# Alternating two score passes of an attention stage pass by pass, and drawing its first projections into the stage before

## Chip, cores, metric

One NeuronCore of a Trainium2 chip runs the whole program. The metric is the device time of one execution in microseconds (us); where a number below is a time on the trace, it counts from the start of the span.

## What is computed

`x` is 32 sequences of 64 tokens of width 128, `ctx_1024` has the same shape. Two decoder layers, each an attention block, a cross attention block and a feed-forward block, each with a residual and a layer norm:

```python
x = _layernorm(x + _L0_attn_ref(x, ...))        # stage 0, a state-space mixer
x = _layernorm(x + _L0_xattn_ref(ctx_1024, ctx_1024, x, ...))   # stage 1
x = _layernorm(x + _L0_ffn_ref(x, ...))         # stage 2, routed experts
x = _layernorm(x + _L1_attn_ref(x, ...))        # stage 3, window attention
x = _layernorm(x + _L1_xattn_ref(x, ctx_1024, ...))   # stage 4
x = _layernorm(x + _L1_ffn_ref(x, ...))         # stage 5, routed experts
```

Stage 4, which the change is about:

```python
def _L1_xattn_ref(x, mem, Wq, Wkv, Wout, bout):     # 16 heads of depth 8, mem = ctx_1024
    q = x @ Wq
    xc = jnp.concatenate((mem, x), axis=1)          # 64 + 64 keys
    k, v = jnp.split(xc @ Wkv, 2, axis=-1)
    dots = jnp.einsum('bhid,bhjd->bhij', q, k) * scale      # per head
    dots = jnp.where(j_idx > i_idx + mem_len, -jnp.inf, dots)
    out = jnp.einsum('bhij,bhjd->bhid', softmax(dots), v)
    return out @ Wout + bout
```

## The kernel before

Activations lie transposed in SBUF (128 features on the partitions, 2048 tokens along them). Each engine has its own hand-written instruction order, and semaphores tie the engines together. Stages 0 to 3 go over four chunks of 512 tokens: `run` calls a `front` for a chunk, which is handed the norm pieces of the chunk before (`hook`) and early pieces of the chunk after (`nxt`). Stage 4 goes over 16 pairs of sequences (`PAIRS`) and 8 halves of a chunk (`HALVES`, four sequences each), one pair per iteration `i` of the loops `stage4` that PE, ACT and DVE each have.

What PE does for a pair `k` in stage 4, with its lines:

- `scores4(k, half)`: queries on the output partitions. Depth is 8, so four heads share a group `g` of 32 partitions; a matmul has 32 rows (group `g`) and 64 output columns (L2097, float32, 256 elements moved). Half 0 takes groups 0 and 1, half 1 groups 2 and 3; both write banks 0 and 1. Eight matmuls of 32 x 32 in bf16 then add the mask (L2104). DVE takes the row maxima (`maxima4`, L1418), splits them in two bf16 parts (`split4`), PE turns them (`turn4`, L2148), ACT copies them.
- `scores_by_key4(k)`: the same scores once more, keys on the output partitions, 32 rows and 128 columns each (L2116, float32, 256 elements moved), groups 0 to 3, banks 2, 3, 5, 6; eight masks of 32 x 32 (L2122, bf16, 512 elements).
- `less_max4(k)` (L2130) takes the maxima off, ACT's `exps4` (L852) makes the exponentials, `pv4(k)` (L2158, L2162) multiplies with the values and sums.
- Once in two iterations each: `k_project4` (L2070) and `q_project4` (L2074), or `v_project4` (L2080). ACT copies the keys (`k_copy4`, L831) and spreads them by head (`k_by_head4`, L837, four activations).

Each float32 matmul stands in the trace as two passes, so a count x16 is eight matmuls. An iteration of PE before:

```python
for i in range(PAIRS + 2):
    scores4(i, 0); scores_by_key4(i - 1)
    k_project4(i // 2 + 1) or v_project4(i // 2)
    q_project4(i // 2 + 1)          # even i
    scores4(i, 1); less_max4(i - 1); pv4(i - 2); turn4(i)
```

`k_project4` and `pv4` share bank 4, so `pv4` waits in an even iteration until ACT has copied the keys; and `k_copy4(h)` itself waits for `s_t4` of `4 * (2 * h - 2)`, that is until `less_max4(i - 1)` of the same iteration, since the two halves in `k4` are by then still being read. `s_t4` counts the last `less_max4` matmul of each group.

Stage 4 opens on PE with the last norm pieces of stage 3 (`tail3`: L2054, L2057), then `k_project4(0)`, `q_project4(0)`; ACT then copies and spreads the keys, and DVE fills `xcat` (`inputs4`) and copies the queries (`q_copy4`). `keep_warm` is six plain bf16 matmuls without use (L2169). POOL sets the value and maxima buffers to zero (L567, L568) and spreads the queries by head (L576).

Of the kernel before, what the change touches and what calls it, by code (L numbers as in the profile page):

```python
# [24 lines left out]
P = 128  # L25
# [17 lines left out]
def _program(nc, ctx, dram, out, where_c, where_w):  # L43
# [115 lines left out]
    def run(eng, fronts, pres, tails):  # L159
# [3 lines left out]
        for front, pre, tail in zip(fronts, pres, tails):  # L163
# [3 lines left out]
            front(NCH - 1, lambda part: tail(NCH - 2, part), nothing)  # L167
# [187 lines left out]
    xcat = take(2 * CHUNK).rearrange("p (b i t) -> p b i t", b=SEQS, i=2)  # L355
# [5 lines left out]
    vx4 = vx4_all.rearrange("p (b j g r) -> p b j g r", b=SEQS, j=4, g=4)  # L361
    max4_all = take(2 * SEQ)
    max4 = max4_all.bitcast(BF16).rearrange("p (i g r) -> p i g r", i=2, g=4)
    maxT4 = [take(SEQ).bitcast(BF16) for _ in range(2)]
# [14 lines left out]
    by_key = [bank[n] for n in (2, 3, 5, 6)]  # L379

# [110 lines left out]
    def _(pool):  # L491
# [73 lines left out]
        def stage4():  # L565
            pool.wait_ge(s_w2, 9 * NCH)
            pool.memset(vx4_all, 0.0).then_inc(s_z4, 1)  # L567
            pool.memset(max4_all, 0.0).then_inc(s_z4, 1)  # L568
            pool.wait_ge(s_wvs, 3 * NCH)
# [10 lines left out]
        run(pool, [front0, front1, front2, front3], [no_pre, no_pre, no_pre, pre3], [tail0, tail1, tail2, tail3])  # L580
# [3 lines left out]
    def _(act):  # L584
# [243 lines left out]
        def k_copy4(h):  # L828
            wait(act, s_k4, h + 1)
            wait(act, s_t4, 4 * (2 * h - 2))  # L830
            act.activation(k4[:, half_rows(h), :], bank[4][:].rearrange("p (b t) -> p b t", b=4), ACT.Copy).then_inc(s_kx4, 1)  # L831

        def k_by_head4(h):
            wait(act, s_kx4, 5 * h + 1)
            wait(act, s_s4, 2 * (2 * h - 2))
            for j in range(4):
                act.activation(kx4[:, half_rows(h), j, :], k4[:, half_rows(h), :], ACT.Copy, scale=const("inner")[:, j:j + 1])\  # L837
# [10 lines left out]
        def exps4(k):  # L848
            wait(act, s_pv4, k - 1)
            for g in range(4):  # L850
                wait(act, s_t4, 4 * k + g + 1)
# [6 lines left out]

        def stage4(hook):
            act.wait_ge(s_z4, 2)  # L860
            k_copy4(0)
            k_by_head4(0)
            hook(1)
            for i in range(PAIRS + 2):
# [7 lines left out]
                if i in VAR_AT4:  # L872
                    tail4(VAR_AT4[i], 2)
                if 1 <= i <= PAIRS:
# [3 lines left out]
                if i in OUT_AT:  # L878
                    tail4(OUT_AT[i], 1)
# [79 lines left out]
        stage5(stage4(run(act, [front0, front1, front2, front3], [no_pre, pre1, pre2, pre3], [tail0, tail1, tail2, tail3])))  # L959
# [1590 lines left out]
```

## Time and profile before

| what | value |
|---|---|
| time of three runs, median (lowest to highest) | 873.44 us (872.77 to 874.19) |
| time of the profiled execution | 873.73 us |
| its span, first to last instruction | 871.9 us |
| granted TensorE clock, mean over the span | 0.968 |
| PE busy | 785.4 us, 90% of the span |
| DVE busy | 492.0 us, 56% |
| ACT busy | 404.9 us, 46% |
| POOL busy | 110.6 us, 13% |
| share of PE in the chain that ended last | 70% |
| stage 3 / stage 4 / stage 5 begin near | 447 / 538 / 693 us |

The profiled execution is 1.8 us longer than its span and 0.3 us above the median. Busy time of PE adds overlapping passes once only; matmuls on different tiles of the array run beside each other, so the mean time of one pass times their number is more than the busy time.

### The profile page before, as it was taken

What the parts mean: (1) busy time and instruction counts of PE and PEld (TensorE: products, weight loads), DVE (VectorE), ACT (ScalarE), POOL (GpSimd) and SP (SyncE); (2) the same over time, 40 slices, a digit from 0 to 9 for tenths busy, and PEclk for the clock granted to TensorE, in tenths of its full rate; (3) what the DMA queues carried; (4) which work ended last, traced back from release to release, by engine and by line L of the source; (5) the groups of instructions that cost most, each with busy time, mean ns of one, the idle gap of its engine ahead of it and who ended that gap; (6) DMA issues with size and microseconds to landing.
All of it is one profiled execution on the core that took longest, in us unless ns stands there. A gap on an engine that the chain in (4) does not pass through costs nothing.

```text
span 871.9 us, 17126 instructions
## 1 busy us (share of the span) xinstructions
PE 785.4 (90%) x6680; PEld 396.7 (45%) x6681; DVE 492.0 (56%) x1166; ACT 404.9 (46%) x735; POOL 110.6 (13%) x107
## 2 busy tenths in 40 slices
PE   6999999997988869999986867899999899999996
PEld 4445354444555533433324444455656544443332
DVE  1543323324888876566448773365666466646662
ACT  3737354554566652333431332355545344554454
POOL 1270221211000000000003445121110000000000
PEclk9999999999899998999997998899999899999998
DMA  9400000000000000000000000000000000000000
GB/s 359 170 2 1 1 0 0 1 2 1 2 2 1 1 2 0 0 1 0 0 1 1 1 0 0 2 3 3 3 3 3 2 0 1 1 1 0 13 12 24
DMA packets 2372, 13.51 MB, mean 15 GB/s; under 512 B 256, under 2 KB 256, under 8 KB 1664
## 3 DMA queue, kind: packets, MB, share of 16 engines
q1 hardware_dynamic: 2304, 12.56, 3.6%
q8 instruction: 47, 0.77, 0.3%
q14 instruction: 21, 0.17, 0.1%
HBM read 11.51 MB, written 1.05 MB: 14 GB/s over the span
## 4 chain that ended last, share of the span: by engine, by line
PE 70%; DVE 13%; ACT 8%; issue 7%; DMA 1%; DVEq 0%; POOL 0%; ACTq 0%; SPq 0%
PE bank L1726 6%; PE bank L2097 4%; PE bank L2338 4%; PE bank L1952 3%; PE bank L2264 3%; PE bank L1764 3%; PE bank L2317 3%; PE bank L2274 3%; PE bank L1777 3%; PE bank L1968 3%; PE bank L1957 3%; PE bank L2116 2%; PE bank L2158 2%; PE bank L121 2%; DVE sb_rowmax L1099 2%
## 5 line engine op out<-in xcount | busy, mean ns | idle before, releaser
L1726 PE MATMUL bank<-sb_xT,sb_arena 128*128 128x512 f32 (+1 forms) x128 | 63.1, 626 | 3.5 <-ACT sb_arena L605 2.5
L1418 DVE TENSOR_REDUCE sb_rowmax<-bank 128x4 f32<-128x512 f32 x64 | 41.1, 684 | 33.8 <-PE bank L2104 33.1
L605 ACT ACTIVATE sb_arena<-bank 128x512 f32<-128x512 f32 x64 | 37.4, 597 | 37.6 <-PE bank L1726 37.5
L1030 DVE TENSOR_TENSOR sb_arena<-bank,sb_arena 128x512 f32<-128x512 f32 x32 | 22.1, 690 | 50.2 <-PE bank L1777 49.9
L757 ACT ACTIVATE sb_arena<-bank 128x512 f32<-128x512 f32 x36 | 21.4, 596 | 55.6 <-PE bank L1952 54.1
L513 POOL TENSOR_TENSOR sb_arena<-sb_la,sb_consts 128x1024 f32<-128x1024 f32 x16 | 30.6, 1920 | 112.2 <-PE bank L1764 88.8
L1952 PE MATMUL bank<-sb_xT,sb_w 128*128 128x512 f32 (+1 forms) x72 | 40.7, 648 | 0.0
L1726 PEld LDWEIGHTS bank<-sb_xT,sb_arena 128*128 128x128 f32 x128 | 22.4, 194 | 37.3 <-ACT sb_arena L605 21.9
L852 ACT ACTIVATE sb_arena<-bank 128x512 f32<-128x512 f32 x64 | 33.0, 605 | 13.3 <-PE bank L2130 13.3
L2097 PE MATMUL bank<-sb_arena 32*64 32x256 f32 x512 | 35.8, 395 | 3.0 <-ACT sb_arena L837 2.9
L1646 DVE TENSOR_TENSOR sb_arena<-sb_arena,bank 128x512 f32<-128x512 f32 x32 | 21.0, 683 | 29.7 <-PE bank L2321 22.0
L1957 PE MATMUL bank<-sb_xT,sb_w 128*128 128x512 f32 (+1 forms) x72 | 37.7, 605 | 0.0
L1968 PE MATMUL bank<-sb_arena,sb_w 128*128 128x512 f32 x72 | 37.6, 614 | 0.0
L648 ACT ACTIVATE sb_arena<-bank 128x512 f32<-128x512 f32 x32 | 18.7, 597 | 39.1 <-PE bank L1764 39.0
L1311 DVE TENSOR_TENSOR sb_arena<-sb_arena,bank 128x512 f32<-128x512 f32 x32 | 21.9, 686 | 25.0 <-PE bank L1957 16.3
L714 ACT ACTIVATE sb_arena<-sb_arena 128x512 f32<-128x512 f32 x32 | 20.1, 630 | 33.0 <-DVE sb_arena L1104 33.0
L1863 PE MATMUL bank<-sb_arena 128*64 128x256 f32 x256 | 34.5, 398 | 0.7 <-ACT sb_arena L672 0.5
L2338 PE MATMUL bank<-sb_arena,sb_w 128*128 128x512 f32 x64 | 34.9, 635 | 0.0
L918 ACT ACTIVATE sb_arena<-bank,sb_w 128x512 f32<-128x512 f32 x32 | 21.3, 687 | 27.4 <-PE bank L2317 27.4
L2041 PE MATMUL bank<-sb_arena,sb_consts 128*128 128x128 f32 x192 | 25.3, 294 | 8.3 <-POOL sb_arena L546 6.6
L1764 PE MATMUL bank<-sb_arena,sb_consts 128*128 128x512 f32 x64 | 32.7, 592 | 0.0
L2317 PE MATMUL bank<-sb_xT,sb_w 128*128 128x512 f32 x64 | 32.3, 597 | 0.0
(344 smaller groups left out, 1640.3 us busy)
## 6 DMA issues: line engine op xcount, KB each, us to landing
sb_w<-w SPq DMA_DIRECT2D x1, 2646.5 KB, 25.6
sb_consts<-consts SPq DMA_DIRECT2D x1, 1812.0 KB, 14.4
sb_w<-w SPq DMA_DIRECT2D x1, 1736.0 KB, 19.4
sb_w<-w SPq DMA_DIRECT2D x1, 1175.0 KB, 9.2
sb_arena<-w SPq DMA_DIRECT2D x2, 512.0 KB, 4.1
sb_ctxT<-ctx SPq DMA_DIRECT2D x1, 1024.0 KB, 16.4
out<-sb_xT SPq DMA_DIRECT2D x4, 256.0 KB, 2.5
sb_xT<-x SPq DMA_DIRECT2D x1, 768.0 KB, 10.6
```

Of the source, the lines that this page charges most:

```text
L605: act.activation(V[:, h, :], bank[h % 2][:], ACT.Copy).then_inc(s_vev, 1)
L852: act.activation(probT4[k % 2][:, g].rearrange("p b j q -> p (b j q)"), by_key[g][:], ACT.Exp).then_inc(s_e4, 1)
L1418: dve.tensor_reduce(rowmax4[k % 2][:, 4 * g:4 * g + 4], bank[n][:].rearrange("p (j t) -> p j t", j=4), AX, ALU.max).then_inc(s_mx4, 1)
L1726: pe.matmul(bank[h % 2][:], KT[:, h, :], cols(c), start=True, stop=True).then_inc(s_v, 1)
L1764: pe.matmul(bank[2 + half][:], const("later"), decay[k % 2][:, 8 * half:8 * half + 8, :].rearrange("p h t -> p (h t)"), start=False, stop= ...
L1863: mm = pe.matmul(bank[2 + u % 3][64 * b:64 * b + 64, 256 * gg:256 * gg + 256], qg[:, 2 * (u % 2) + gg, q:q + SEQ], kx[:, 2 * k + b].rearra ...
L1952: pe.matmul(bank[n % 2][:], w1v[:, i, :], cols(c), start=True, stop=True).then_inc(s_g2, 1)
L1957: pe.matmul(bank[2 + n % 2][:], w3v[:, i, :], cols(c), start=True, stop=True).then_inc(s_u2, 1)
L1968: pe.matmul(bank[5][:], w2v[:, (n - 3) % 9, :], hid[(n - 2) % 3], start=(n == 2), stop=(n == 10))\
L2097: mm = pe.matmul(scored[64 * b:64 * b + 64, :, at], q4[rows(g), q:q + SEQ], kx4[rows(g), b0 + b, :, at], start=(part == 0), stop=True, ski ...
L2317: pe.matmul(up_bank(c, i)[:], f1v[:, i, :], cols(c), start=True, stop=True).then_inc(s_f1, 1)
L2338: pe.matmul(bank[3][:], f2v[:, i, :], hid5[i % 4], start=(i == 0), stop=False).then_inc(s_f2, 1)
```

## The change

Four things. (1) `scores_by_key4(k)` is gone; `scores4(i, half)` now issues the pair `i` in the one form and the pair `i - 1` in the other, in turn: for each of two parts, four matmuls of 32 x 64 on two row groups, then two of 32 x 128 on the other two row groups. The masks of both follow. (2) The keys have three buffers instead of two halves of one, and `k_copy4` waits for an older `less_max4`. (3) `k_project4(0)`, `q_project4(0)`, their copies and both `inputs4` stand in the last chunk of stage 3, and `scores4(0, 0)` ahead of `tail3`; POOL's zeroing stands in the first chunk of stage 3. (4) Buffers move so that this is free of overlaps; the orders of groups for masks, `less_max4` and `exps4` become 2, 3, 0, 1; `tail4(.., 1)` on ACT stands ahead of `exps4`.

```diff
-            front(NCH - 1, lambda part: tail(NCH - 2, part), nothing)
+            front(NCH - 1, lambda part: tail(NCH - 2, part), opening if front is fronts[-1] else nothing)
...
-    k4 = take(SEQS * P).rearrange("p (b t) -> p b t", b=SEQS)
+    k4 = [ap.rearrange("p (b t) -> p b t", b=4) for ap in (take(4 * P), sb("k4_second", [P, 4 * P])[:], sb("k4_third", [P, 4 * P])[:])]
...
+    KEY_GROUPS = (2, 3, 0, 1)
+    projected_q4 = [bank[6], bank[5]] + [bank[7]] * (2 * NCH - 2)
...
@@ POOL, front3, first chunk @@
+                pool.wait_ge(s_w2, 9 * NCH)
+                pool.memset(vx4_all, 0.0).then_inc(s_z4, 1)
+                pool.memset(max4_all, 0.0).then_inc(s_z4, 1)
                 pre3(0, 4)
@@ ACT @@
         def k_copy4(h):
             wait(act, s_k4, h + 1)
-            wait(act, s_t4, 4 * (2 * h - 2))
-            act.activation(k4[:, half_rows(h), :], bank[4][:].rearrange("p (b t) -> p b t", b=4), ACT.Copy).then_inc(s_kx4, 1)
+            wait(act, s_t4, 4 * (2 * h - 4))
+            act.activation(k4[h % 3], bank[4][:].rearrange("p (b t) -> p b t", b=4), ACT.Copy).then_inc(s_kx4, 1)
...
+        def opening4(piece):
+            if piece == 3:
+                k_copy4(0)
+                k_by_head4(0)
@@ DVE @@
+        def opening4(piece):
+            if piece == 0:
+                inputs4(0)
+            if piece == 2:
+                q_copy4(0)
+            if piece == 3:
+                inputs4(1)
@@ PE @@
         def scores4(k, half):
-            groups = (2 * half, 2 * half + 1)
-            b0 = 2 * (k % 4)
-            wait(pe, s_kx4, 5 * (k // 2) + 5)
-            wait(pe, s_qc4, k // 2 + 1)
-            wait(pe, s_mx4, 4 * k + 2 * half)
+            groups, key_groups = (2 * half, 2 * half + 1), KEY_GROUPS[2 * half:2 * half + 2]
+            b0, e0 = 2 * (k % 4), 2 * ((k - 1) % 2)
+            if k < PAIRS:
+                wait(pe, s_kx4, 5 * (k // 2) + 5)
+                wait(pe, s_qc4, k // 2 + 1)
+                wait(pe, s_mx4, 4 * k + 2 * half)
+            if k > 0:
+                wait(pe, s_kx4, 5 * ((k - 1) // 2) + 1)
+                wait(pe, s_qx4, 4 * ((k - 1) // 2) + 4)
+                wait(pe, s_e4, 4 * (k - 1) - 2 + 2 * half)
             for part in range(2):
                 at = slice(SEQ * part, SEQ * part + SEQ)
+                if k < PAIRS:
+                    for g in groups:
...
+                            pe.matmul(scored[64 * b:64 * b + 64, :, at], q4[rows(g), q:q + SEQ], kx4[rows(g), b0 + b, :, at],
+                                      start=(part == 0), stop=True, skip_group_check=(part == 1))
+                if k > 0:
+                    for g in key_groups:
+                        pe.matmul(by_key[g][:, 256 * part:256 * part + 256], k4[(k - 1) // 2 % 3][rows(g), e0 + part, :],
+                                  qx4[rows(g), 2 * ((k - 1) % 4) + part].rearrange("p j q -> p (j q)"), start=(part == 0),
+                                  stop=True, skip_group_check=(part == 1))
...
         def turn4(k):
             wait(pe, s_mb4, 2 * k + 2)
+            if k == 0:
+                wait(pe, s_resid, 4 * NCH)
...
+        def opening4(piece):
+            if piece == 1:
+                pe.wait_ge(s_w[4], 16)
+                pe.wait_ge(s_c3, 3 * NCH)
+                k_project4(0)
+                q_project4(0)
...
         def stage4(hook):
-            hook(0)
...
             for i in range(PAIRS + 2):
-                if i < PAIRS:
+                if i <= PAIRS:
                     scores4(i, 0)
-                if 1 <= i <= PAIRS:
-                    scores_by_key4(i - 1)
+                if i == 0:
+                    hook(0)
```

**The order on PE, iteration 3 of stage 4.** The names in it: L2097 is a score matmul of 32 x 64, L2104 its mask, L2116 a by-key matmul of 32 x 128, L2122 its mask, L2080 the value projection, L2130 `less_max4`. Before:

```order
L2097 MATMUL bank<-sb_arena 64x4x64 x8
L2104 MATMUL bank<-sb_consts 32x4x64 x8
L2116 MATMUL bank<-sb_arena 128x256 x8
L2122 MATMUL bank<-sb_consts 32x512 x8
L2080 MATMUL bank<-sb_w,sb_arena 128x128 x4
L2097 MATMUL bank<-sb_arena 64x4x64 x8
L2104 MATMUL bank<-sb_consts 32x4x64 x8
L2130 MATMUL bank<-sb_arena,sb_consts 128x2x64 x16
L2158 MATMUL bank<-sb_arena 32x64 x32
L2162 MATMUL bank<-sb_arena,sb_consts 32x128 x16
```

In the changed kernel the same stretch reads as follows (L2115 is the score matmul, L2119 the by-key one, L2126 and L2135 their masks, L2091 the value projection):

```order
L2115 MATMUL bank<-sb_arena 64x4x64 x4
L2119 MATMUL bank<-sb_arena,sb_k_second 128x256 x2
L2115 MATMUL bank<-sb_arena 64x4x64 x4
L2119 MATMUL bank<-sb_arena,sb_k_second 128x256 x2
L2126 MATMUL bank<-sb_consts 32x512 x4
L2135 MATMUL bank<-sb_consts 32x4x64 x8
L2091 MATMUL bank<-sb_w,sb_arena 128x128 x4
L2115 MATMUL bank<-sb_arena 64x4x64 x4
L2119 MATMUL bank<-sb_arena,sb_k_second 128x256 x2
L2115 MATMUL bank<-sb_arena 64x4x64 x4
L2119 MATMUL bank<-sb_arena,sb_k_second 128x256 x2
L2126 MATMUL bank<-sb_consts 32x512 x4
```

The matmuls are the same in number. The eight by-key matmuls that stood in one run behind the first half now stand in four runs of two, each between runs of four score matmuls, and the shape changes with each run.

**The order on PE where stage 3 ends.** Before, from the last chunk's norm pieces on (L2041 spreads window weights, L121 is the variance, L2054 and L2057 are `tail3`, L2070 and L2074 the first projections):

```order
L2054 MATMUL bank<-sb_xT,sb_consts 128x512
L2057 MATMUL bank<-sb_arena,sb_w 128x512 x3
L2041 MATMUL bank<-sb_arena,sb_consts 128x128 x24
L121 MATMUL bank<-sb_sq,sb_consts 128x512
L2054 MATMUL bank<-sb_xT,sb_consts 128x512
L2057 MATMUL bank<-sb_arena,sb_w 128x512 x3
L2070 MATMUL bank<-sb_arena,sb_w 128x512
L2074 MATMUL bank<-sb_xT,sb_w 128x256
L2097 MATMUL bank<-sb_arena 64x4x64 x8
L2104 MATMUL bank<-sb_consts 32x4x64 x8
```

And in the change (L2052 spreads the window weights, L2065 and L2068 are `tail3`, L2081 and L2085 the projections):

```order
L2068 MATMUL bank<-sb_arena,sb_w 128x512 x3
L2052 MATMUL bank<-sb_arena,sb_consts 128x128 x12
L2081 MATMUL bank<-sb_arena,sb_w 128x512
L2085 MATMUL bank<-sb_xT,sb_w 128x256
L2052 MATMUL bank<-sb_arena,sb_consts 128x128 x12
L121 MATMUL bank<-sb_sq,sb_consts 128x512
L2115 MATMUL bank<-sb_arena 64x4x64 x8
L2135 MATMUL bank<-sb_consts 32x4x64 x8
L2065 MATMUL bank<-sb_xT,sb_consts 128x512
L2068 MATMUL bank<-sb_arena,sb_w 128x512 x3
L2081 MATMUL bank<-sb_arena,sb_w 128x512
L2085 MATMUL bank<-sb_xT,sb_w 128x256
```

The two projections moved to the middle of the window weights of the last chunk, and the first scores ahead of `tail3`.

**The order on ACT there.** Before (L126, L135, L138 are norm pieces, L831 copies the keys, L837 spreads them):

```order
L126 ACTIVATE sb_sq<-sb_resid 128x512
L135 ACTIVATE sb_lnv<-bank,sb_eps_ln 128x512
L138 ACTIVATE sb_rstd<-sb_lnv 128x512
L831 ACTIVATE sb_arena<-bank 128x512
L837 ACTIVATE sb_arena<-sb_arena,sb_consts 128x4x128 x4
L126 ACTIVATE sb_sq<-sb_resid 128x512
L831 ACTIVATE sb_arena<-bank 128x512
```

In the change (L834 copies the keys, L840 spreads them):

```order
L126 ACTIVATE sb_sq<-sb_resid 128x512
L834 ACTIVATE sb_arena<-bank 128x512
L840 ACTIVATE sb_arena<-sb_arena,sb_consts 128x4x128 x4
L135 ACTIVATE sb_lnv<-bank,sb_eps_ln 128x512
L138 ACTIVATE sb_rstd<-sb_lnv 128x512
L126 ACTIVATE sb_sq<-sb_resid 128x512
L834 ACTIVATE sb_k_second<-bank 128x512
```

Copy and spreading of the first keys moved ahead of the norm of the last chunk but one.

## Rows read from the trace of the kernel before

**Rows 1.** The page: busy time by engine, share of the span, instructions
```profile
PE 785.4 (90%) x6680; PEld 396.7 (45%) x6681; DVE 492.0 (56%) x1166; ACT 404.9 (46%) x735; POOL 110.6 (13%) x107
```

**Rows 2.** Busy time of the engines 588 to 680 us, PE PEld DVE ACT POOL, clock, DMA
```profile
588.00:680.00 92.00, 88.11 (x2124) 56.46 (x2119) 55.72 (x109) 47.49 (x109) 9.31 (x16) 1.00 0.01 3
```

**Rows 3.** The chain over two iterations of stage 4: start us, us, what
```profile
585.10 0.61 ACT sb_arena L831
...
585.75 1.10 PE bank L2158 x64
...
587.88 1.02 PE bank L2097 x16
588.90 0.23 PE bank L2104 x8
589.13 1.07 PE bank L2116 x16
590.21 0.34 PE bank L2122 x8
590.55 1.09 PE bank L2080 x8
591.64 1.02 PE bank L2097 x16
...
597.96 1.06 PE bank L2070 x2
599.02 0.43 PE bank L2074 x2
```

**Rows 4.** Timeline of PE, where shapes change: start us, us, engine, line, output and inputs
```profile
588.29 0.61 PE L2097 MATMUL bank<-sb_arena 32*64 32x256 f32 x8
588.83 0.30 PE L2104 MATMUL bank<-sb_consts 32*32 32x256 bf16 x8
...
592.59 0.30 PE L2104 MATMUL bank<-sb_consts 32*32 32x256 bf16 x8
592.82 0.40 PE L2130 MATMUL bank<-sb_arena,sb_consts 32*128 32x128 bf16 x16
```

**Rows 5.** Timeline of PE, 548 to 600 us, six useless bf16 matmuls
```profile
551.30 1.47 PE L2169 MATMUL bank<-sb_consts 128*128 128x512 bf16 x6
```

**Rows 6.** Waits from 553 to 680 us: who waited for whom, total us, times, longest
```profile
PE bank L2158 <- ACT sb_arena L831: 5.0, 6, 0.8
```

**Rows 7.** Timeline of DVE, the maxima of one half
```profile
589.21 1.29 DVE L1418 TENSOR_REDUCE sb_rowmax<-bank 128x4 f32<-128x512 f32 x2
```

**Rows 8.** Timeline of all engines, 515 to 548 us, end of stage 3, start of stage 4
```profile
526.15 5.52 PE L2041 MATMUL bank<-sb_arena,sb_consts 128*128 128x128 f32 x48
...
533.31 1.13 PE L2054 MATMUL bank<-sb_xT,sb_consts 128*128 128x512 f32 x2 [0.78 <-ACT sb_lnv L135]
...
534.27 2.74 PE L2057 MATMUL bank<-sb_arena,sb_w 128*128 128x512 f32 x6
...
538.35 1.10 PE L2070 MATMUL bank<-sb_arena,sb_w 128*128 128x512 f32 x2 [1.34 <-DVE sb_arena L1404]
...
539.54 0.60 ACT L831 ACTIVATE sb_arena<-bank 128x512 f32<-128x512 f32 x1 [5.62 <-PE bank L2070]
...
540.17 2.56 ACT L837 ACTIVATE sb_arena<-sb_arena,sb_consts 128x512 f32<-128x512 f32 x4
...
542.78 1.98 PE L2097 MATMUL bank<-sb_arena 32*64 32x256 f32 x16 [2.91 <-ACT sb_arena L837]
```

**Rows 9.** Timeline of PE, 548 to 600 us, second run of scores
```profile
550.04 1.09 PE L2097 MATMUL bank<-sb_arena 32*64 32x256 f32 x16
```

**Rows 10.** Timeline, POOL's zeroing, and DVE's products without and with POOL busy
```profile
533.68 3.52 POOL L567 MEMSET sb_arena<- 128x4096 f32 x1
...
449.23 3.70 DVE L1343 TENSOR_TENSOR sb_arena<-sb_arena 128x512 f32<-128x512 f32 x6 [1.66 <-ACT sb_arena L779]
...
464.26 6.30 DVE L1343 TENSOR_TENSOR sb_arena<-sb_arena 128x512 f32<-128x512 f32 x6 [1.91 <-ACT sb_arena L779]
```

More of the change, by code:

```diff
@@ L157, in is_last, with run @@
         return isinstance(c, int) and c == NCH - 1
-    def run(eng, fronts, pres, tails):
+    def run(eng, fronts, pres, tails, opening):
         hook = nothing
@@ L354, in _program @@
     attn4 = [take(CHUNK), sb("attn4_odd", [P, CHUNK])[:]]
-    xcat = take(2 * CHUNK).rearrange("p (b i t) -> p b i t", b=SEQS, i=2)
+    maxT4 = [take(SEQ).bitcast(BF16) for _ in range(2)]
+    take = carve(11840)
     q4 = take(CHUNK)
     qx4 = take(4 * CHUNK).rearrange("p (b j q) -> p b j q", b=SEQS, j=4)
-    k4 = take(SEQS * P).rearrange("p (b t) -> p b t", b=SEQS)
+    k4 = [ap.rearrange("p (b t) -> p b t", b=4) for ap in (take(4 * P), sb("k4_second", [P, 4 * P])[:], sb("k4_third", [P, 4 * P])[:])]
     kx4 = take(SEQS * 4 * P).rearrange("p (b j t) -> p b j t", b=SEQS, j=4)
@@ L361, in _program @@
     vx4 = vx4_all.rearrange("p (b j g r) -> p b j g r", b=SEQS, j=4, g=4)
+    xcat = take(2 * CHUNK).rearrange("p (b i t) -> p b i t", b=SEQS, i=2)
     max4_all = take(2 * SEQ)
     max4 = max4_all.bitcast(BF16).rearrange("p (i g r) -> p i g r", i=2, g=4)
-    maxT4 = [take(SEQ).bitcast(BF16) for _ in range(2)]
     rden4 = rms_l[:, 0:P]
@@ L579, in _ @@
         setup_pool()
-        run(pool, [front0, front1, front2, front3], [no_pre, no_pre, no_pre, pre3], [tail0, tail1, tail2, tail3])
+        run(pool, [front0, front1, front2, front3], [no_pre, no_pre, no_pre, pre3], [tail0, tail1, tail2, tail3], nothing)
         stage4()
@@ L849, in exps4 @@
             wait(act, s_pv4, k - 1)
-            for g in range(4):
-                wait(act, s_t4, 4 * k + g + 1)
+            for n, g in enumerate(KEY_GROUPS):
+                wait(act, s_t4, 4 * k + n + 1)
                 act.activation(probT4[k % 2][:, g].rearrange("p b j q -> p (b j q)"), by_key[g][:], ACT.Exp).then_inc(s_e4, 1)
@@ L873, in stage4 @@
                     tail4(VAR_AT4[i], 2)
+                if i in OUT_AT:
+                    tail4(OUT_AT[i], 1)
                 if 1 <= i <= PAIRS:
@@ L958, in _ @@
         setup_act()
-        stage5(stage4(run(act, [front0, front1, front2, front3], [no_pre, pre1, pre2, pre3], [tail0, tail1, tail2, tail3])))
+        stage5(stage4(run(act, [front0, front1, front2, front3], [no_pre, pre1, pre2, pre3], [tail0, tail1, tail2, tail3], opening4)))
     @block.vector
@@ L1693, in _ @@
         setup_dve()
-        stage5(stage4(run(dve, [front0, front1, front2, front3], [no_pre, pre1, pre2, pre3], [tail0, tail1, tail2, tail3])))
+        stage5(stage4(run(dve, [front0, front1, front2, front3], [no_pre, pre1, pre2, pre3], [tail0, tail1, tail2, tail3], opening4)))
     @block.tensor
@@ L2095, in scores4 @@
                     for b in range(2):
[L2096 to L2124 removed]
+                        for h in range(2):
+                            o = 64 * b + 32 * h
+                            mm = pe.matmul(scored[o:o + 32, :, SEQ:], eye32[rows(g)],
+                                           late_key[rows(g), h].unsqueeze(1).to_broadcast([32, 4, SEQ]), start=False, stop=True,
+                                           skip_group_check=True)
+                mm.then_inc(s_s4, 1)
         def less_max4(k):
@@ L2128, in less_max4 @@
             for j in range(4):
-                for g in range(4):
+                for g in KEY_GROUPS:
                     mm = pe.matmul(by_key[g][:].rearrange("p (b j q) -> p b j q", b=2, j=4)[:, :, j, :],
@@ L2386, in _ @@
         setup_pe()
-        stage5(stage4(run(pe, [front0, front1, front2, front3], [no_pre, pre1, pre2, pre3], [tail0, tail1, tail2, tail3])))
+        stage5(stage4(run(pe, [front0, front1, front2, front3], [no_pre, pre1, pre2, pre3], [tail0, tail1, tail2, tail3], opening4)))
 def _layouts(np, a):
```

69 lines of the change are left out of this document (18 added, 51 removed).

## Prediction

> **What bounds the kernel now.** I read the page first: PE is busy for 90% of the span, DVE for 56% [rows 1], and the page's chain that ended last lies on PE for most of its length. Then the steady part of stage 4 alone, 588 to 680 us: PE busy 88.1 of 92 us at the full granted clock, DVE 55.7, ACT 47.5 [rows 2]. So what the change does to PE's own time there counts in full. The chain over two iterations [rows 3] shows the pieces end to end: score run 1.02, its masks 0.23, by-key run 1.07, its masks 0.34, a projection, the second score run 1.02. The one wait of any size is ACT's copy of the keys, 0.61.
>
> **What a run of small matmuls is made of.** Two passes of 256 elements in float32 that follow without a change of shape take 0.43, the last row of [rows 3], so a pass streams in 0.215. The 16 passes of the score run are four rounds on four tiles (two row groups, two column halves): 0.86, and 0.16 over. The by-key run is four rounds on four row groups: 0.86, and 0.21 over [rows 3]. Six plain bf16 passes of 512 elements take 1.47 including the tail of the last [rows 5], about 0.22 each; so the eight masks of 256 elements (0.11) and of 512 (0.22) all run beside each other and leave 0.12 over in 0.23 and 0.34 [rows 3]. Every run pays 0.12 to 0.21 for being a new shape.
>
> **Does a change of shape wait for tiles that it doesn't use?** This decides the case. At 592.59 the masks are on row groups 2 and 3. The next shape, 32 x 128, begins with group 0, which nothing had used since before the run at 591.64, yet it starts 0.23 after the masks, just as late as the by-key run behind the masks of half 0 (588.83 to 589.07), which needs the tiles that they hold [rows 4]. The eight take 0.30 together, most of it the way through the array; the last starts 0.02 after the first and streams for 0.11, so the new shape starts 0.10 after the whole array is through. I looked at every change of shape in the trace, several hundred: none starts earlier than about 0.09 after the stream before it ends. The Trainium skill, page TensorEngine Tiling (Array Packing), section Key Properties, has the same: changing the tiling mode, not merely the tile, drains TensorE. By that rule the trace agrees, and it speaks against this change.
>
> **Term 1, the alternated passes.** A half of `scores4` in iterations 1 to 15 is now two parts of: eight score passes, two rounds on four tiles, 0.43 + 0.16 = 0.59; then four by-key passes, two rounds on two tiles, 0.43 + 0.21 = 0.64. Half of the four row groups stand idle in each run. Both sets of masks are 32 x 32 and go together: 0.34. A half is 2 x (0.59 + 0.64) + 0.34 = 2.80, a pair 5.60. Before, a pair was 1.02 + 0.23 + 1.07 + 0.34 + 1.02 + 0.23 = 3.91 [rows 3], 62.6 for 16 pairs. Now: the first iteration has scores alone, 2 x 1.25 = 2.5; fifteen mixed ones, 84.0; iteration 16 has by-key alone but in two runs, 2 x (0.86 + 0.21 + 0.34) = 2.8. Sum 89.3, **+26.7**. Nothing hides it, since PE is the bound.
>
> **Term 2, the third key buffer.** The copy of the keys waited for `less_max4` and `pv4` for the copy, six times, 5.0 us idle [rows 6]. Now the copy only needs the projection, 2 us or more ahead, and ACT is free then. **-5.0.** The wait that could come in its place is the exponentials of the pair before; they follow `less_max4` at 0.6 each (the copy of that shape takes 0.60 [rows 8]), and the first two are asked for only after both runs of `pv4`, the first of which alone takes 1.10 [rows 3], and `turn4`: no wait.
>
> **Term 3, less cover for the maxima.** The second half of a pair writes the banks that DVE reads for the first. The maxima end 1.67 after the first mask starts (588.83 to 590.50) [rows 4, 7]; with twelve masks and the semaphore I take 1.85. By-key matmuls used to lie between the halves; now there is 0.34 for the masks and a projection: 1.09 in odd iterations, 1.06 + 0.43 in even ones [rows 3]. So odd iterations wait 0.4, even ones not. Most odd ones have a norm piece there; iterations 3 and 5 have none. **+0.9.** Behind that wait on PE stand the second half, `less_max4` and `turn4`, so it counts in full.
>
> **Term 4, the opening.** Before, the first scores start at 542.78, behind `tail3`, the projections, the copy (0.60) and four spreading activations (2.56) [rows 8]. Now the projections stand in the middle of L2041, whose 48 passes take 5.52 from 526.15: after 24 of them, 528.9. They delay the second 24 by 1.06 + 0.43 = 1.5; L121 then ends near 533.9. ACT starts the copy near 529.9 and is done near 533.1, ahead of that. So the first scores start near 534.0 at the full clock: 8.8 earlier. From there to the second run of scores PE had 7.3 (542.78 to 550.04 [rows 8, 9]), part of it at the lower clock (the first run took 1.98 for the usual 1.02). Now: scores and masks 1.25, `tail3` 1.0 + 2.6, without the last pass's tail [rows 8], projections 1.5, `keep_warm` 1.4 [rows 5] and some 0.15 of waits: 7.9. Net **-8.1**. Bounds: -9 (no stretch at the lower clock and no waits) and -3 (DVE's value products, the copy of the queries and two `inputs4` pile up in the last chunk, or the new order brings a lower clock itself). I take the value from the added rows; it is nearest to them.
>
> **Term 5, POOL's zeroing** (3.52) moves to 446 us, beside the first products of stage 3. Six of those took DVE 3.70 alone and 6.30 with POOL busy [rows 10]; some 1.5 us of overlap at that rate would cost 0.6; a memset reads nothing, so it may cost 0: **+0.5**, bounds 0 and 1.5. The old place of the zeroing was beside PE's work: no gain. The extra buffers, the order of groups and the place of `tail4(.., 1)` cost nothing: same instructions, and ACT has half its time free.
>
> **Sum.** The profiled execution took 873.7 (span 871.9 and 1.8 around it), 0.3 above the median. 26.7 - 5.0 + 0.9 - 8.1 + 0.5 = +15.0, so 888.7 against the execution, **888.4** against the median.
>
> **Rivals.** (a) *Tiles of different shape do overlap when their row groups are disjoint.* The group orders 2, 3, 0, 1 are laid out for it. A half would be four rounds with one change, 0.86 + 0.21, and 0.34: 1.41. A pair 2.82; stage 4's runs 2.5 + 15 x 2.82 + 2.8 = 47.6, -15.0, and with the other terms -26.7: **846.7**. It decides if a by-key pass starts within some 0.03 of the score pass issued ahead of it. The same page and section of the Trainium skill says that different tiles can load and multiply in parallel; both rules are stated and the trace shows each, the second only within one shape. For it: nothing but that no float32 pair of shapes on disjoint groups is in the trace. Against: rows 5. Chance 0.15. (b) *A change between 32 x 64 and 32 x 128 is cheap*, since both have 32 rows: it waits for the stream but the 0.16 and 0.21 shrink to the 0.10 that follows every stream. 120 runs, some 0.08 less each: -9, **879**. Chance 0.08. (c) *The opening pays little, or the emptier array brings the lower clock back.* At the lower clock a stretch costs as much again as it takes (the run of scores 1.98 for 1.02 [rows 8, 3]); a stretch of some 7 us more at that clock costs 3.5, the opening at its bound another 5: **893 to 897**. Chance 0.15. (d) Gains and losses cancel: 0.02.
>
> **How the numbers follow.** Forecast 0.60, its own span 883 to 893. A measurement of this kernel can tell 0.2% (1.7 us) from no change. Faster is (a) and a little of (d), 0.16; within 0.2% 0.02; slower all else, 0.82. The range 875 to 899 holds the forecast, (b), (c); outside lie (a), (d) and 0.03 of tails.
>
> **What would show it.** The score passes in fours and the by-key passes in twos, each run starting only when the one before is through: a by-key run 0.59 after the score run, the next score run 0.64 later, a half 2.8 long. An even and an odd iteration together some 2.6 longer than before (3.4 more for two pairs, 0.8 less for one copy). ACT's copy of the keys gone from the chain. First scores near 534, the second run near 542. It is wrong if by-key passes start inside the score run's rounds, or if other stages move by over 1 us.

## The result, and the profile after

| | before | after |
|---|---|---|
| device time, median (lowest to highest) | 873.82 us (872.77 to 877.2), 4 runs | 897.89 us (895.27 to 901.77), 4 runs |
| profiled execution / its span | 873.73 / 871.9 us | 895.27 / 893.5 us |
| granted TensorE clock, mean over the span | 0.968 | 0.968 |
| PE busy | 785.4 us, 90% | 811.1 us, 91% |

The ratio is 1.0272, with a 95% interval of 1.0224 to 1.0321: slower by 2.7%. The forecast was 888.4 with a range to 899; the median lies inside it, 9.5 above the forecast. It lies outside the forecast's own span of 883 to 893, and also above the 893 to 897 of rival (c). The profiled execution is the fastest of the four; the other three took 896.71, 899.08 and 901.77 us with clocks of 0.963, 0.963 and 0.960.

The page of the changed kernel, busy time by engine (to be read beside [rows 1]):

```profile
PE 811.1 (91%) x6680; PEld 402.2 (45%) x6681; DVE 493.5 (55%) x1166; ACT 405.8 (45%) x735; POOL 111.0 (12%) x107
```

PE gained 25.7 us of busy time with the same instructions; DVE, ACT and POOL did not move. So most of the added time is not PE waiting for another engine: the same passes of PE lie less beside each other.

The chain of waits of the changed kernel over an odd and the following even iteration (start us, us, what), beside [rows 3]:

```profile
569.90 0.64 issue
570.53 0.66 PE bank L2115 x8
...
575.77 0.59 PE bank L2115 x8
576.37 0.63 PE bank L2119 x4
577.00 0.59 PE bank L2115 x8
577.59 0.63 PE bank L2119 x4
578.22 0.22 PE bank L2126
578.44 0.02 PE bank L2135 x7
...
578.47 1.13 PE bank L2081 x2
...
580.03 0.13 issue
```

The same half by the starts of its matmuls, from the timeline of PE:

```profile
575.70 0.66 PE L2115 MATMUL bank<-sb_arena 32*64 32x256 f32 x8
576.29 0.70 PE L2119 MATMUL bank<-sb_arena,sb_k_second 32*128 32x256 f32 x4
```

The next two runs start at 576.93 and 577.52, the masks at 578.15 and the projection at 578.47. A half is 0.59, 0.63, 0.59, 0.63 and 0.32 for the masks, 2.77 in all against a forecast of 2.80, and so, within 0.01, is every other half between 565 and 675 us. (The chain starts a piece where the one before ends, at 575.77, so it shows 2.70 and 0.25 for the masks, and 0.66 for the first run of a half that follows a wait.) Where [rows 3] had one score run of 1.02 and one by-key run of 1.07, there are now four runs, each of which begins when the one before is through. The `issue` piece of 0.64 at 569.90 is new: the second half of the pair waits there until DVE has read the banks that it will write (DVE's side is in the rows below).

Timeline of the changed kernel, DVE and PE around that wait (start us, us, engine, line, output and inputs, idle time before and its releaser):

```profile
568.93 1.29 DVE L1424 TENSOR_REDUCE sb_rowmax<-bank 128x4 f32<-128x512 f32 x2 [1.55 <-PE bank L2135]
...
570.53 0.66 PE L2115 MATMUL bank<-sb_arena 32*64 32x256 f32 x8 [0.64 <-issue]
```

DVE reads the first half's scores from 568.93 to 570.22. The value projection (568.74 to 569.90) covers the first 0.97 of that, and the second half starts 0.3 after DVE's end. Here the first half is followed by nothing but the projection; before, the by-key run stood there too.

Timeline of the changed kernel at the end of stage 3 and the opening of stage 4, beside [rows 8, 9]:

```profile
527.40 1.02 PE L2081 MATMUL bank<-sb_arena,sb_w 128*128 128x512 f32 x2
...
529.09 2.56 ACT L840 ACTIVATE sb_arena<-sb_arena,sb_consts 128x512 f32<-128x512 f32 x4
...
532.32 1.09 PE L2115 MATMUL bank<-sb_arena 32*64 32x256 f32 x16
...
539.79 1.09 PE L2115 MATMUL bank<-sb_arena 32*64 32x256 f32 x16
```

The projections stand in the middle of the window weights, and ACT has copied and spread the keys by 531.65, before PE asks for them. The first scores start at 532.32 for 542.78 before, the second run at 539.79 for 550.04. That is 10.25 earlier, of which 1.81 is older: stage 3 itself began at 444.87 instead of 446.68. The opening paid 8.4, of which 3.4 is the stretch at the lower clock that it had before.

The granted clock of stretches of the changed kernel (window, its length, busy time of PE, PEld, DVE, ACT and POOL, clock, DMA):

```profile
543.00:553.00 10.00, 8.34 (x103) 3.96 (x103) 3.32 (x8) 6.67 (x15) 0.00 (x0) 1.00 0.00 1
553.60:560.40 6.80, 6.80 (x39) 2.65 (x37) 1.29 (x2) 0.60 (x1) 0.00 (x0) 0.50 0.01 2
588.00:680.00 92.00, 89.91 (x1753) 49.41 (x1749) 45.61 (x89) 41.20 (x92) 9.31 (x16) 0.98 0.01 3
683.30:690.10 6.80, 6.80 (x137) 4.31 (x137) 1.64 (x4) 2.06 (x4) 0.00 (x0) 0.50 0.01 2
```

Two stretches of 6.8 us ran at 0.50, that is at 1.2 GHz, and one of 3.4 us more lies inside 588 to 680. Both long ones follow idle time of PE: 1.7 of the 10 us before 553, and a wait of 1.73 at 680.2. The short one, at 608.2, does not: PE was busy for 4.73 of the 5 us ahead of it. Before, the stretch from 588 to 680 ran at 1.00 throughout [rows 2]; a stretch like the long ones lay in the opening, where the run of scores took 1.98 [rows 8], and a short one in iteration 2:

```profile
563.20:566.60 3.40, 3.40 (x23) 1.28 (x16) 0.85 (x2) 0.00 (x0) 0.00 (x0) 0.50 0.00 0
```

### The profile page after: what moved, and what is told of

Its sections match the earlier page's. It is cut to its first block, busy times and chain, and to the rows that moved or that the text cites. A ratio compares the mean times of both kernels' runs of the same rounds, so it can differ in the third digit from the quotient of the medians.

```text
span 893.5 us, 17165 instructions
## 1 busy us (share of the span) xinstructions
PE 811.1 (91%) x6680; PEld 402.2 (45%) x6681; DVE 493.5 (55%) x1166; ACT 405.8 (45%) x735; POOL 111.0 (12%) x107
## 4 chain that ended last, share of the span: by engine, by line
PE 69%; DVE 15%; issue 8%; ACT 7%; DMA 1%; DVEq 0%; POOL 0%; ACTq 0%; SPq 0%
PE bank L1737 6%; PE bank L2119 5%; PE bank L2115 4%; PE bank L2354 4%; PE bank L1963 3%; PE bank L2280 3%; PE bank L1775 3%; PE bank L2333 3%; PE bank L2290 3%; PE bank L1788 3%; PE bank L1979 3%; PE bank L1968 3%; DVE sb_rowmax L1105 2%; PE bank L121 2%; PE bank L2269 2%
## 5 line engine op out<-in xcount | busy, mean ns | idle before, releaser
L760 ACT ACTIVATE sb_arena<-bank 128x512 f32<-128x512 f32 x36 | 21.4, 596 | 55.7 <-PE bank L1963 54.1
L2115 PE MATMUL bank<-sb_arena 32*64 32x256 f32 x512 | 42.7, 406 | 4.2 <-issue 3.0
L2052 PE MATMUL bank<-sb_arena,sb_consts 128*128 128x128 f32 x192 | 25.9, 297 | 9.3 <-POOL sb_arena L550 7.6
L579 POOL TENSOR_TENSOR sb_arena<-sb_arena,sb_consts 128x256 f32<-128x256 f32 x32 | 19.1, 628 | 115.0 <-PE bank L2144 112.3
```

The costliest lines, as they stand in the source:

```text
L2115: pe.matmul(scored[64 * b:64 * b + 64, :, at], q4[rows(g), q:q + SEQ], kx4[rows(g), b0 + b, :, at], start=(part == 0), stop=True, skip_gro ...
```

## The experiments

All times are compared with runs of the kernel before on the same chip: 873.03 us (13 runs, 868.45 to 876.57) for the first four, 873.92 us (11 runs, 868.36 to 877.13) for the others. Diffs are against the changed kernel.

**1. The same passes in one shape.** Does the change of shape cost the time, or the alternation? The by-key matmul of 128 columns is cut into two of 64, so that it has the shape of the score matmul. There are 256 passes more, and no change of shape before the masks of a half.

```diff
                     for g in key_groups:
-                        pe.matmul(by_key[g][:, 256 * part:256 * part + 256], k4[...][rows(g), e0 + part, :], ...)
+                        for u in range(2):
+                            pe.matmul(by_key[g][64 * u:64 * u + 64, 256 * part:256 * part + 256],
+                                      k4[...][rows(g), e0 + part, 64 * u:64 * u + 64], ...)
```

> The changed kernel, but each by-key matmul of 32 x 128 is cut into two of 32 x 64, so scores and by-key passes have one shape and still lie on disjoint row groups; twice as many by-key passes. Theory (the price is the change of shape, and tiles of one shape overlap across all row groups): a mixed half is four rounds on eight tiles and one mask run, 0.86 + 0.16 + 0.05 + 0.34 = 1.4 us instead of the 2.77 of the changed kernel, 30 halves: 41 us less than the changed kernel's 898, about 857 us, ratio to before 0.98. Rival (no more than four passes stream at a time whatever their tiles): 32 passes in eight rounds, 2.2 us a half, about 881 us. Rival (disjoint row groups don't overlap at all): 3 us a half and over, 905 us or more.

Measured: 855.86 us (854.14 to 859.63), ratio 0.9818 (0.9764 to 0.9872): 42 us faster than the changed kernel and 17 faster than the one before, as the theory had it. Both rivals are out. Timeline of PE in this kernel, one half (L2115 is a score pass, L2120 a by-key pass):

```profile
576.27 0.45 PE L2115 MATMUL bank<-sb_arena 32*64 32x256 f32 x4
576.30 0.45 PE L2120 MATMUL bank<-sb_arena,sb_k_third 32*64 32x256 f32 x4
576.54 0.40 PE L2115 MATMUL bank<-sb_arena 32*64 32x256 f32 x4
576.57 0.39 PE L2120 MATMUL bank<-sb_arena,sb_k_third 32*64 32x256 f32 x4
...
577.32 0.39 PE L2128 MATMUL bank<-sb_consts 32*32 32x512 bf16 x4
...
577.65 1.16 PE L2091 MATMUL bank<-sb_w,sb_arena 128*128 128x128 f32 x8
```

The by-key passes start 0.03 after the score passes, inside their round, and the next round of four and four comes 0.27 later. All eight tiles stream together. A half takes 1.38, from 576.27 to 577.65, against 2.77 with two shapes. Of the 20 halves between 568 and 645 us 14 take 1.38; the other six hold pauses of PE and take 1.69 to 2.37. The data, the row groups, the banks and the order are the same; the only thing changed is that a tile has 64 columns and not 128 (and that there are two passes for one). This is the rival (a) of the prediction in all but its premise: the row groups do overlap, but only in one shape. In the words of the Trainium skill, page TensorEngine Tiling (Array Packing), section Key Properties, different tiles can run in parallel, and changing the tiling mode drains TensorE; the runs agree with both, and show that the second comes first.

**2. Fewer changes of shape.** Per half all score passes, then all by-key passes: one change inside a half where there were three.

```diff
-                if k > 0:
+            if k > 0:
+                for part in range(2):
                     for g in key_groups:
                         pe.matmul(by_key[g][:, 256 * part:256 * part + 256], ...
```

> The changed kernel, but inside a half all score passes go first and then all by-key passes: two runs of small matmuls instead of four, still on half of the row groups each. Theory: 1.02 + 1.07 + 0.34 = 2.43 us a half instead of 2.77, 30 halves, 10 us less than the changed kernel: about 888 us, ratio 1.016. Rival (the changes of shape themselves are cheap and the idle row groups are the whole price): 897 us, no difference from the changed kernel.

Measured: 892.65 us (892.04 to 893.41), ratio 1.0239 (1.0192 to 1.0285). The chain of this kernel shows the two runs of a half in place of four:

```profile
590.66 1.09 PE bank L2115 x16
591.75 1.06 PE bank L2120 x8
592.82 0.22 PE bank L2127
```

1.09 and 1.06, that is 2.15 for the 2.44 of the four runs (0.59, 0.63, 0.59, 0.63). An even iteration takes 9.15 (from one `turn4` to the next) against 9.87, which is 0.36 less per half. Over 30 halves that is 10.8 us, but the median fell by 5.2 only. The rest is in the clock:

```profile
553.80:570.90 17.10, 16.62 (x194) 9.34 (x198) 5.14 (x12) 3.94 (x10) 2.33 (x4) 0.50 0.01 2
```

17.1 us at 1.2 GHz in one stretch, where the changed kernel had 6.8 in that place. That costs (17.1 - 6.8) / 2, some 5 us more. So the price of a change of shape is confirmed as such (the rival expected no difference), and half of what two fewer of them gave was taken back by the clock. Why this order has more of the lower clock stays open.

**3. The by-key run whole again.** The alternation alone is undone: eight by-key matmuls in one run behind half 0, with their masks and waits, as before. The opening and the third key buffer stay.

```diff
+            if k > 0 and half == 0:
+                for part in range(2):
+                    for g in key_groups:
+                        pe.matmul(by_key[g][:, 256 * part:256 * part + 256], ...
...
-                if i <= PAIRS:
+                if i < PAIRS:
                     scores4(i, 1)
```

> The changed kernel, but the by-key pass is one run over all four row groups behind the first half's scores and masks again, as before the change; the opening, the third key buffer and everything else of the change stay. Theory: the alternation costs all of the loss, so this is faster than before by the opening (8 to 10 us) and the key copy (some 4 of its 5 us, the rest goes to the wait for the maxima ahead of the turn in even iterations): 859 to 862 us, ratio 0.985. Rival (the opening or the new key buffers are part of the loss): 870 us or more.

**4. The same, and the old wait of the copy.** On top of run 3 the copy of the keys waits again for the `less_max4` of the same iteration.

```diff
-            wait(act, s_t4, 4 * (2 * h - 4))
+            wait(act, s_t4, 4 * (2 * h - 2))
```

> As whole_key_run, with the copy of the keys waiting for the same less_max4 as before the change. Theory: the six waits of 0.9 us for ACT's copy come back, less the 0.2 each that the maxima would have cost: 4 us more than whole_key_run, 864 to 866 us, ratio 0.990. Rival (the third buffer saves nothing, as another wait is as late): the same time as whole_key_run within 1 us.

Measured: run 3 took 860.78 us (858.89 to 863.22), ratio 0.9863 (0.9816 to 0.991), and run 4 took 867.5 us (859.37 to 869.8), ratio 0.9926 (0.9891 to 0.996). Run 3 is as expected; run 4 lies 1.5 above its 864 to 866, and its intervals with run 3 overlap a little, so their difference is read from the profiled executions below (867.1 and 863.22). Both are faster than before, so the alternation alone is what made the change slower: it accounts for 37 us between run 3 and the changed kernel, more than the whole loss. (It brings with it the shorter cover for the maxima of term 3.) Some 30 of them are the passes and the waits for the maxima (steps 1 and 3 below), and 8 the clock: run 3's spans at 0.971 miss 24.9 us of it, the changed kernel's at 0.963 miss 33.

The difference of 3 and 4 is the third key buffer. The chain of run 4 in an even iteration:

```profile
595.43 0.61 ACT sb_k_second L834
...
596.08 1.10 PE bank L2175 x64
```

and that of run 3 in the same place:

```profile
596.77 0.40 DVE sb_arena L1435
...
597.20 0.55 DVE sb_arena L1437
...
597.79 0.23 PE bank L2165
```

In run 4 ACT's copy of 0.61 stands on the chain, as in [rows 3]. In run 3 it is gone, and DVE's split of the maxima stands there (L1435, L1437), for which `turn4` waits. An even iteration takes 8.72 in run 4, as before, and 8.06 in run 3: 0.66 gained of the 0.83 that the copy cost (5.0 over six [rows 6]). The split is slow just there. Timeline of run 3, DVE and POOL:

```profile
595.95 2.33 POOL L579 TENSOR_TENSOR sb_arena<-sb_arena,sb_consts 128x256 f32<-128x256 f32 x4 [13.14 <-PE bank L2145]
...
596.77 0.39 DVE L1435 CAST sb_arena<-sb_rowmax 128x16 bf16<-128x16 f32 x1
597.20 0.54 DVE L1437 TENSOR_TENSOR sb_arena<-sb_rowmax,sb_arena 128x16 bf16<-128x16 f32 x1
```

The two small instructions take 0.39 and 0.54 while POOL spreads the queries (L579); in odd iterations, without POOL, they take 0.17 each. The kernel before had the same slow pair in its even iterations (0.39 and 0.54), hidden behind the wait for the copy. The Trainium skill, page GPSIMD Engine Reference, section Specifications, says that POOL and DVE share their access to SBUF, and contend where a DVE instruction has two SBUF inputs or runs in a 2-port mode; L1437 has two inputs and grew most. L1435 has one and more than doubled as well; whether it ran in a 2-port mode no trace here shows. That POOL's work is the cause is shown by run 7 below.

**5. Filling the idle time ahead of the slow stretches.** The changed kernel with six `keep_warm` matmuls ahead of `turn4(1)` and seven between the halves of iteration 14. The two waits added there let them write to bank 4, and no result is touched.

```diff
+                if i == 14:
+                    wait(pe, s_o4, 12)
+                    keep_warm(7, bank[4])
                 if i <= PAIRS:
                     scores4(i, 1)
...
+                if i == 1:
+                    wait(pe, s_vx4, 4)
+                    keep_warm(6, bank[4])
                 if i < PAIRS:
                     turn4(i)
```

> The changed kernel with useless bf16 matmuls of 128 x 128 x 512 into bank 4 in the two places where PE waited longest: six ahead of turn4(1) (1.6 us idle) and seven between the halves of iteration 14 (1.7 us idle). They compute nothing and shift nothing if they fit the waits. Theory (PE's low granted clock at 553.6 to 560.4 and 683.3 to 690.1 of the changed kernel's trace follows from those two waits): both stretches of 6.8 us at the lower clock go, 3 us each, so about 892 us instead of 898, and iterations 2 and 14 last some 10.4 and 9.8 us instead of 12.9 and 12.8. Rival (the lower clock comes from elsewhere, such as the emptier array): the stretches stay or come a little later, 897 us or more.

Measured: 894.14 us (888.27 to 896.0), ratio 1.0223 (1.0185 to 1.0261). The granted clock in five stretches of this kernel:

```profile
553.60:560.40 6.80, 6.28 (x71) 2.77 (x69) 3.49 (x9) 2.82 (x6) 0.00 (x0) 1.00 0.01 2
588.50:598.70 10.20, 10.20 (x145) 6.49 (x148) 2.93 (x6) 2.85 (x8) 0.00 (x0) 0.50 0.01 3
612.40:615.80 3.40, 3.40 (x14) 1.90 (x13) 1.27 (x2) 0.78 (x4) 0.00 (x0) 0.50 0.02 5
653.30:656.70 3.40, 3.40 (x24) 2.34 (x22) 1.29 (x2) 0.98 (x5) 0.00 (x0) 0.51 0.00 0
683.30:690.10 6.80, 6.64 (x78) 2.70 (x71) 2.18 (x4) 0.05 (x1) 0.00 (x0) 1.00 0.01 4
```

Where the lower clock had been, at 553.6 and 683.3, it is now 1.00, and iterations 2 and 14 take 10.02 and 9.62 instead of 12.94 and 12.80. But 17.0 us at 0.50 turn up at 588.5, 612.4 and 653.3, places that had been free of it or had 3.4. The sum within stage 4's iterations is the 17.0 of before the edit, in the profiled executions. PE had hardly been idle ahead of the new places:

```profile
583.50:588.50 5.00, 4.73 (x128) 2.73 (x117) 2.92 (x6) 4.63 (x9) 2.33 (x4) 1.00 0.01 3
553.00:680.00 127.00, 123.65 (x2221) 67.11 (x2218) 60.11 (x118) 54.63 (x120) 13.96 (x24) 0.93 0.01 2
```

So the theory held for the two places, and its rival has a share in the rest: idle time of PE is not needed for a stretch at the lower clock. The profiled execution is the slowest of the six here, and that of the changed kernel the fastest of its four. The medians, 894.14 and 897.89, lie 3.8 apart, nearer to the 892 of the theory than to the 897 of the rival, but their intervals overlap (1.0185 to 1.0261 and 1.0224 to 1.0321). Whether the filling gained time in this kernel stays open.

**6 to 8. Further on the faster form.** Run 6 is run 1 with the edit of run 5. Run 7 is run 1 with POOL's spreading held back until DVE's split is done; run 8 has both.

```diff
                 wait(pool, s_t4, 4 * (2 * h - 2))
+                wait(pool, s_mb4, 2 * (2 * h - 1) if h >= 2 else 0)
```

> The kernel with one shape for both passes and the same useless matmuls. Its profile had 3.4 us at the lower clock in iteration 2 and 3.4 us in iteration 14. Theory: both go, 1.7 us each: 852 to 853 us against 856. Rival: no difference, 856 us.

> The kernel with one shape, and POOL's spreading of the queries waits until DVE has split the maxima of the same iteration, instead of running beside it. In even iterations the two instructions of the split took 0.36 and 0.55 us beside POOL, against 0.17 and 0.17 in odd ones. Theory (POOL holds DVE up, and turn4 waits for it): six iterations shorter by up to 0.5 us each, 853 to 854 us against 856. Rival (the turn is covered by pv4 anyway): no difference.

> The kernel with one shape, with the useless matmuls and the later POOL work together. Theory: the two savings add, 850 to 852 us, ratio to before 0.975. Rival: they hit the same wait, 853 us or more.

| run | us, median (lowest to highest) | ratio (95% interval) |
|---|---|---|
| 6, one shape, filled | 851.2 (849.33 to 855.11) | 0.9761 (0.9716 to 0.9806) |
| 7, one shape, POOL late | 856.8 (854.91 to 859.28) | 0.9817 (0.9773 to 0.9861) |
| 8, one shape, both | 853.7 (849.39 to 857.24) | 0.9769 (0.9729 to 0.9808) |

Run 6 has the lowest median, 22.7 us below the kernel before. It lies 4.7 below run 1, more than the 3.4 of its theory, and their intervals overlap, so the gain of the filling is likely but not shown by the times. The window from 553 to 680 us in it (busy time of PE, PEld, DVE, ACT, POOL, clock):

```profile
553.00:680.00 127.00, 115.14 (x3166) 73.84 (x3165) 80.71 (x170) 69.52 (x150) 13.96 (x24) 1.00 0.01 3
```

There is no lower clock in these 127 us at all, so in this execution, unlike in run 5, the filled stretches did not come back elsewhere in the iterations; run 8's has none there either, but 6.8 us of it at 669.6, behind them. From 553 to 657 us, in the iterations alone, PE was idle for 6.9 of 104 us here and for 3.1 in run 5, which had the lower clock three times there: idle time of PE alone does not decide it. Another difference between the two is that in run 6 eight tiles work at a time and in run 5 four or two; that this is the cause was not tried by itself. Run 7 was a miss: the split did fall to 0.175 for each instruction, and the time did not move (856.8 for 855.86, almost the same interval). Run 8's 853.7 is its rival's figure. With the halves short, other waits stand behind the split; in run 1's chain they are these (start us, us, what):

```profile
577.16 1.94 ACT sb_arena L840 x3
...
589.86 0.93 issue
590.78 0.47 PE bank L2176 x18
```

The first stands ahead of a second half, for which PE was idle 0.64 until 579.44. The chain names ACT's spreading of keys, done at 579.10, but these are the keys of the next iteration. What the program makes a second half wait for are the maxima of the first, and DVE was done with them at 579.13 (1.29 from 577.84). The half starts 0.31 after that, as it does in the changed kernel. The other is a pause of PE of 0.93 in the middle of `pv4`. PE is busy for 115.1 of 127 us in run 6, and it no longer sets the end at each point. Runs 6 and 8 can't be told apart, their intervals overlap for the most part.

## Why the prediction was right, and by how much each step was off

The sign and the mechanism were right: slower, by the drained changes of shape, less what the copy and the opening give. The size was less so: the larger errors below (steps 2 and 3 and the lower clock, 8.4 together) all lie on the side of the loss. That the median is inside the range is owed to its upper end, drawn for rival (c), and in part to luck. By the stretches of the profiled executions (`turn4(0)` to `turn4(15)` took 126.87 before and 158.42 after, 31.5 more):

| step | forecast | measured | how |
|---|---|---|---|
| 1, alternated passes | +26.7 | +25.5 | a pair 5.54 for 3.92 by the starts of its matmuls, 1.61 x 15; 1.4 for iteration 16 |
| 2, third key buffer | -5.0 | -4.0 | 0.66 x 6 from runs 3 and 4 |
| 3, less cover for the maxima | +0.9 | +4.5 | rest of the 31.5: less 24.1 of step 1 and 6.8 of the clock, and the 4.0 of step 2 put back |
| 4, opening | -8.1 | -8.4 | 10.25 less 1.81 of stages before |
| 5, zeroing on POOL | +0.5 | 0 | six products 3.70 beside the memset |
| lower clock elsewhere | 0 | +3.8 | -1.8 before stage 3, +6.8 in the iterations, -1.2 left over behind them |
| sum, of the span | +15.0 | +21.4 (21.6 measured) | |

The row of step 3 and the last part of the clock are remainders, so that the sum comes out is no proof of it. Over the whole span the two profiled executions had nearly the same granted clock, as the 3.4 that step 4 took away is 3.4 of the clock too: nearly all of the 21.6 is work and waits.

**Step 1** stood on [rows 4]: a new shape starts only after the whole array is through, though the tiles it needs are free. It held in each of the 90 places where scores and by-key passes now follow each other inside a half: in 87 the new shape starts 0.30 after the last pass of the old one, that is 0.09 after that has streamed (0.215), and the other three lie at the lower clock (0.56). The runs take 0.59 and 0.63 for the 0.59 and 0.64 forecast. Run 1 shows the cause by taking it away, run 2 takes two of the three changes of a half away and gains 0.36. The masks go in 0.32 and not 0.34, which with the 0.01 of the by-key runs is the small miss of this term.

**Step 2**: "no wait" was wrong. I looked for what holds ACT next, and not for what holds PE next. With the copy off the chain `turn4` waits for the split, which POOL makes slow in just these iterations. Runs 3 and 4 isolate it: 0.66 of 0.83. "No wait" had been worked out for the exponentials alone.

**Step 3** was mis-sized, the largest error of the sum. I gave odd iterations 0.4, even ones none, and let the norm pieces cover the rest. The trace has 0.64 in an odd iteration without a norm piece and 0.13 to 0.2 in even ones; and I overlooked that iteration 14 has no projection at all between its halves. The prediction took 1.85 from the first mask to the second half; it is 2.10 in iteration 3 (568.43 to 570.53). Iteration 14 waits longest:

```profile
681.99 0.66 PE L2115 MATMUL bank<-sb_arena 32*64 32x256 f32 x8 [1.73 <-issue]
...
683.21 1.11 PE L2115 MATMUL bank<-sb_arena 32*64 32x256 f32 x8
684.25 1.22 PE L2119 MATMUL bank<-sb_arena 32*128 32x256 f32 x4
```

1.73 of wait, and at 683.21 and 684.25 the next two runs take 1.11 and 1.22 for the usual 0.66 and 0.70: the clock fell behind it. The lengths of the iterations, less 1.61 for step 1 and less the clock, share out the 4.5: 1.3 in iteration 14, 0.9 each in 3 and 5, 0.8 in the six even ones together, and 0.1 to 0.2 each in most other odd ones. This is also why an even and an odd iteration together came 2.9 longer (19.91 for 16.99) where the odd one has a norm piece and 3.7 (19.81 for 16.13) where it has none, against the 2.6 that the prediction named.

**Step 4** came as worked out from the added rows: first scores forecast 534.0, second run 542; they came at 532.3 and 539.8, with the 1.8 from before stage 3 in both. Run 4 is nearest to the opening alone, since its copy waits as before and its by-key run is whole. It gained 5.5 us against before, not 8.4. The clock of one stretch of it says where the rest is:

```profile
554.40:561.20 6.80, 6.80 (x52) 2.93 (x44) 1.29 (x2) 0.20 (x2) 0.00 (x0) 0.50 0.00 0
```

6.8 us at 0.50, where the kernel before had 3.4 (563.2 to 566.6): iteration 2 took 11.88 for 10.31. Another 1.6 were lost before stage 3, with 3.4 us at the lower clock near 59 us; the second run of scores came 94.4 after stage 3 began, for 103.4 before, so the opening itself gained 9.0. Of that 3.4 is lower clock that the opening no longer has, and half of this came back in iteration 2. The rest, some 5 us, is waiting taken away.

**Step 5**: DVE's six products beside the memset, to be read against [rows 10]:

```profile
445.10 3.51 POOL L560 MEMSET sb_arena<- 128x4096 f32 x1 [127.65 <-PE bank L1979]
...
447.43 3.70 DVE L1349 TENSOR_TENSOR sb_arena<-sb_arena 128x512 f32<-128x512 f32 x6 [1.66 <-ACT sb_arena L782]
```

3.70, as without POOL. The memset ends at 448.61, so it lies beside the first 1.2 us of them, some 1.5 forecast. The bound of 0 was the right end.

**The lower clock** is the term that the sum lacked, and rival (c) had at 0.15. It added to the forecast case rather than taking its place. Where PE is the bound, the time lost to it is the span times what is missing of the clock: 871.9 x 0.032 = 27.9 us before, 893.5 x 0.032 = 28.6 in the profiled execution, and about 895 x 0.037 = 33 in those at 0.963. In step 4 I counted the 3.4 us that the opening had lost at the lower clock as won, and it was; but between `turn4(0)` and `turn4(15)` 17.0 us now ran at it where 3.4 had, which costs 6.8. Of the 9.1 that the median lies above the sum (24.1 for 15.0), steps 1 to 5 make 2.6, these 3.8 the next part, and the rest is that most executions lose more to the clock than the profiled one, the fastest.

One sign of being wrong came up: other stages were not to move by over 1 us, and stages 0 to 2 ended 1.81 earlier. The change has no part in them. The trace has 3.4 us less at the lower clock there (1.7 lost), in a stretch that starts at 219, and the profile of run 2, whose stages 0 to 2 are those of the changed kernel, has all 6.8 again from 219.3: it is the clock's difference between executions and not an effect of the edit. Stage 3 has as much lower clock as before, and what follows `turn4(15)` takes 192.1 for 191.8.

Rival (a) at 846.7 was false for this kernel; with one shape it is nearly what was measured (855.86, and 851.2 filled). Rival (b) fell by the same rows as step 1: a change between 32 x 64 and 32 x 128 cost no less than any other. Where the prediction says "Against: rows 5" in (a), the rows that speak against it are [rows 4]; rows 5 has only the useless matmuls.

## What to carry to other kernels

Small matmuls on separate row groups overlapped here only while all of them had one tile shape, columns included; before alternating two kinds of pass, make them one shape (here two matmuls of 64 columns for one of 128, for 256 more passes and half the time of a half that has no pause), and otherwise keep each shape in runs as long as the buffers allow. When a wait is taken off the chain, work out which wait stands next on the engine that is the bound, in every iteration and above all in those that have less filler work than the others. A stretch at the lower clock that an edit removes is not won until the whole profile's clock says so.

## What was not expected of the hardware

- Eight tiles of 32 x 64 on four row groups stream together: four score passes at 576.27, four by-key passes 0.03 later, the next round 0.27 after the first (run 1). I had expected it, if at all, for any shapes.
- The lower clock came back elsewhere: 6.8 and 6.8 us filled away, 10.2, 3.4 and 3.4 in other places in one execution (run 5), with PE busy for 4.7 of the 5 us ahead of the first; with eight tiles at work the same filling left none in the iterations (run 6), though PE was idle for more of them.
- Two instructions of DVE on 16 elements a row take 0.17 each alone, 0.39 and 0.54 beside POOL's products, but DVE's products of 512 elements were not slowed by POOL's memset (six in 3.70).
- PE paused for 0.93 inside `pv4` at 589.86 (run 1) with nothing in the profile that released it. Its cause stays open.
